# A fused cross-attention and routed feed-forward kernel: six small moves between the engines at once

## The reference, cut to what matters

```python
x = x + xattn(layernorm(x), ctx)        # x, ctx: (128 batches, 128 tokens, 256)
x = x + ffn(layernorm(x))
# xattn: 16 heads of 16; q = xn Wq + bq, k = ctx Wk + bk, v = ctx Wv + bv
#        softmax(q k^T / 4) v, then Wo, bo
# ffn:   logits = xn Wr + rb; e = argmax(logits) over 32 experts
#        y = relu(relu(xn W1[e] + b1[e]) W2[e] + b2[e]), hidden size 64
```

## Time and profile before

| | |
|---|---|
| three runs, median | 1183.46 us (1182.79 to 1188.08) |
| the profiled execution, its own time | 1188.65 us |
| its span, first to last instruction | 1186.8 us |
| mean granted TensorE clock | 0.975 of full speed |
| PE, DVE, POOL, ACT busy | 92%, 80%, 74%, 67% |
| block stage | up to about 957 us |
| page stage | about 964 us to the end |

### The profile page before, as it was taken

One profiled execution on the slowest core, in us unless ns is written; L12 is line 12 of the kernel. 1 busy time (PEld: TensorE's weight loads), 2 busy tenths in 40 slices (PEclk: granted clock), 3 DMA queues, 4 the chain that ended last, 5 costly groups with the idle time before them and its releaser, 6 DMA issues. The chain is left out here.

```text
span 1186.8 us, 38807 instructions
## 1 busy us (share of the span) xinstructions
PE 1090.2 (92%) x15164; PEld 817.5 (69%) x15164; DVE 946.0 (80%) x2360; ACT 799.1 (67%) x1860; POOL 875.5 (74%) x1709
## 2 busy tenths in 40 slices
PE   5999999999999999999999999999998539999992
PEld 4676777777777777777777777777776339888772
DVE  5688888888888888888888888888888538777672
ACT  4777777777777777777777777777775326566551
POOL 5467777777777777777777777777776547777776
PEclk9999999999999999999999999999999759999997
DMA  6516222522222222222222222222210146666650
GB/s 217 167 55 144 77 79 83 149 79 77 84 77 73 74 73 79 77 74 74 73 75 81 81 75 74 73 77 81 68 41 34 58 155 202 205 209 205 203 160 12
DMA packets 91282, 120.37 MB, mean 101 GB/s; under 512 B 14096, under 2 KB 74139, under 8 KB 90909
## 3 DMA queue, kind: packets, MB, share of 16 engines
q1 hardware_dynamic: 77278, 84.04, 25.7%
q0 software_dynamic: 13824, 33.85, 7.8%
HBM read 60.61 MB, written 59.31 MB: 101 GB/s over the span
## 5 line engine op out<-in xcount | busy, mean ns | idle before, releaser
L575 DVE TENSOR_REDUCE mx<-m 128x4 bf16<-128x512 f32 x512 | 323.7, 672 | 3.3 <-PE m L790 3.2
L462 ACT ACTIVATE arena<-sc 128x512 f32<-128x512 f32 x512 | 264.6, 603 | 47.1 <-PE sc L814 46.9
L424 POOL DMA_INDIRECT out<-arena x160 | 157.3, 983 | 61.2 <-issue 35.4
L396 POOL DMA_INDIRECT pages<-row,slot_i x128 | 129.7, 1014 | 57.1 <-issue 53.8
L805 PE MATMUL sc<-qk 32*128 32x256 f32 x2048 | 166.6, 396 | 0.7 <-DVE bo_s L680 0.5
L823 PE MATMUL pB<-arena 128*32 128x128 f32 x4096 | 158.6, 277 | 0.6 <-DVE row L584 0.6
L831 PE MATMUL pB<-wo_s,aT 128*128 128x288 f32 x512 | 149.5, 415 | 6.9 <-DVE aT L606 6.9
L823 PEld LDWEIGHTS pB<-arena 128*32 128x32 f32 x4096 | 99.1, 110 | 43.9 <-issue 42.4
L773 PE MATMUL pA<-cHi,wqkv 128*128 128x512 f32 x252 | 119.6, 476 | 9.5 <-DVE wqkv L648 9.5
L773 PE MATMUL pA<-xnT,wqkv 128*128 128x512 f32 x372 | 126.2, 447 | 0.0
L595 DVE STREAM_TRANSPOSE tr<-pB 128x512 f32<-128x512 f32 x128 | 91.5, 714 | 36.8 <-PE pB L823 35.1
(11 more groups left out here) (158 smaller groups left out, 2489.4 us busy)
## 6 DMA issues: line engine op xcount, KB each, us to landing
arena<-pages SPq DMA_DIRECT2D x160, 130.0 KB, 2.5
cT<-ctxT SPq DMA_DIRECT2D x64, 256.0 KB, 3.5
xs<-x_in SPq DMA_DIRECT2D x128, 128.0 KB, 2.2
pages<-empty SPq DMA_DIRECT2D x120, 130.0 KB
pages<-empty SPq DMA_DIRECT2D x1, 5200.0 KB, 19.9
out<-arena POOLq DMA_INDIRECT x160
w2s<-w SPq DMA_DIRECT2D x1, 2080.0 KB
qk<-w SPq DMA_DIRECT2D x1, 2064.0 KB, 8.5
```

Source lines behind the costliest of these rows:

```text
L396: pool.indirect_dma_start(pages, bass.IndirectOffsetOnAxis(slot_i[:, u:u + 1], 0), row[:, q % 4, u, 0:ROW], None, bounds_check=last_slot, ...
L424: pool.indirect_dma_start(out_rows, bass.IndirectOffsetOnAxis(pr[:, r, COL_TOKEN:COL_TOKEN + 1].bitcast(U32), 0), pr[:, r, X0:X0 + D], Non ...
L462: act.activation(pt[:, u % 2, g].rearrange("p i k -> p (i k)"), sc[g][:, :], ACT.Exp).then_inc(S["exp_out"], 1)
L575: ins = dve.tensor_reduce(mx[:, 32 * g:32 * g + 4], mb[i][:, :].rearrange("p (h k) -> p h k", h=4), AX.X, ALU.max)
```

## The change

1. **4+2 projection.** `project` takes a range of its six matmuls. In u=1 and u=2 four of them go ahead of `values` and two after `project_out`; in u=0 and u=3 it stays three and three.
2. **Another bank for the router.** The logits' transpose and the ranks, and what reads them, use sc[0] in place of sc[3]. `logits_transpose` waits for no exponential of its own any more (`values` ahead of it waits for the second), `ranks` for the first.
3. **The router's choice.** `best(s-1)` runs ahead of `residual` in u=1, no longer behind it. `stats1` takes batch 0 in u=0, 1 and 2 in u=1 and 3 in u=3, where it took 0, 1, and then 2 and 3 at the end of u=2.
4. **Inverse sums in PSUM.** `inv` is 16 columns of bank pB.
5. **Rounded context by ScalarE.** `context_hi` replaces GpSimd's cast: in u=0 behind `v_copy`, for block s+2. For block 0 it is ScalarE's first work, for block 1 it is in u=3 of s=-2.
6. **GpSimd's list.** `rstd1` goes to the head of a block, ahead of `scatter`. `slot_sum` writes integers itself (with max, as all but one of the slots' products are zero) into two buffers, so GpSimd's cast goes; `meta` is two instructions and no longer five.

```diff
+        inv = pB[:, 480:496]
...
-                pe.transpose(sc[3][:, 0:P], lgs[:, :], ident).then_inc(S["lgT_done"], 1)
+                pe.transpose(sc[0][:, 0:P], lgs[:, :], ident).then_inc(S["lgT_done"], 1)
...
             def split(q):
-                for c in range(2):
-                    pool.wait_ge(S[f"ld_c{c}"], q * 16 + 16)
-                if q >= 2:
-                    after(pool, "V_done", 4, q - 2, 3)
-                pool.tensor_copy(cHi[:, q % 2], cT[:, :, :]).then_inc(S["ctx_hi"], 1)
                 after(pool, "ctx_hi", 1, q, 0)
...
-                pool.tensor_scalar(expert[:, :], idx[:, :], -1.0, float(E), ALU.mult, ALU.add).then_inc(S["expert_out"], 1)
-                pool.tensor_copy(row[:, q % 4, :, COL_TOKEN].bitcast(I32), tok[:, :])
-                pool.tensor_copy(row[:, q % 4, :, COL_EXPERT].bitcast(I32), expert[:, :]).then_inc(S["meta_out"], 1)
-                pool.tensor_scalar(tok[:, :], tok[:, :], float(QB * P), None, ALU.add).then_inc(S["tok_out"], 1)
+                pool.tensor_scalar(row[:, q % 4, :, COL_TOKEN].bitcast(I32), cst[:, C_TOKEN:C_TOKEN + QB], float(q * QB * P), None, ALU.add)
+                pool.tensor_scalar(row[:, q % 4, :, COL_EXPERT].bitcast(I32), idx[:, :], -1.0, float(E), ALU.mult, ALU.add).then_inc(S["meta_out"], 1)
...
-                pool.tensor_copy(slot_i[:, :], slot[:, :]).then_inc(S["slot_int"], 1)
...
             for s in range(-1, NQ + 2):
+                if live(s + 2):
+                    rstd1(s + 2)
                 if live(s - 2):
-                    slots_as_integers(s - 2)
                     scatter(s - 2)
                 if live(s - 1):
                     rstd2(s - 1)
                     scale_logits(s - 1)
-                if live(s + 2):
-                    rstd1(s + 2)
...
+            def context_hi(q):
+                for c in range(2):
+                    act.wait_ge(S[f"ld_c{c}"], q * 16 + 16)
+                if q >= 2:
+                    after(act, "V_done", 4, q - 2, 3)
+                act.activation(cHi[:, q % 2], cT[:, :, :], ACT.Copy).then_inc(S["ctx_hi"], 1)
...
+                    if s == -2 and u == 3:
+                        context_hi(1)
+                    if u == 0 and s >= 0 and live(s + 2):
+                        context_hi(s + 2)
...
-                dve.tensor_reduce(slot[:, :], t1[:, :, :], AX.X, ALU.add).then_inc(S["slot_out"], 1)
+                dve.tensor_reduce(slot_i[:, q % 2, :], t1[:, :, :], AX.X, ALU.max).then_inc(S["slot_out"], 1)
...
-                    if u < 2 and live(s + 3):
-                        stats1(s + 3, (u,))
+                    if u != 2 and live(s + 3):
+                        stats1(s + 3, ((0,), (1, 2), (), (3,))[u])
...
+                    if u == 1 and live(s - 1):
+                        best(s - 1)
                     if live(q1):
                         residual(q1, u1)
-                    if u == 1 and live(s - 1):
-                        best(s - 1)
-                    if u == 2 and live(s + 3):
-                        stats1(s + 3, (2, 3))
...
-                        project(pq, n, (0, 1) if s < 0 else (0,))
+                        project(pq, n, 0, 6 if s < 0 else (3, 4, 4, 3)[u])
...
                     if u == 1 and s >= 0 and live(s + 1):
-                        after(pe, "exp_out", 16, s, 4 * u + 3)
                         logits_transpose(s + 1)
                     if u == 2 and live(s - 1):
                         if live(s):
-                            after(pe, "exp_out", 16, s, 4 * u + 3)
+                            after(pe, "exp_out", 16, s, 4 * u)
                         ranks(s - 1)
                     if live(q1):
                         project_out(q1, u1)
                     if live(pq) and s >= 0:
-                        project(pq, n, (1,))
+                        project(pq, n, (3, 4, 4, 3)[u], 6)
```

More of the change, by code:

```diff
@@ L120, in build @@
         t1 = sb("t1", [QB, E])
-        slot, slot_i = sb("slot", [QB]), sb("slot_i", [QB], U32)
-        tok, expert = sb("tok", [QB]), sb("expert", [QB])
+        slot_i = sb("slot_i", [2, QB], U32)
         empty = sb("empty", [ROW])
@@ L392, in scatter @@
                     pool.wait_ge(S[f"fill{q % 4}"], q // 4 * 64 + 64)
-                after(pool, "slot_int", 1, q, 0)
+                after(pool, "slot_out", 1, q, 0)
                 after(pool, "meta_out", 1, q, 0)
@@ L430, in _ @@
         def _(act):
+            def context_hi(q):
[4 more added lines that the diff above has]
+                act.activation(cHi[:, q % 2], cT[:, :, :], ACT.Copy).then_inc(S["ctx_hi"], 1)
+            context_hi(0)
             act.wait_ge(S["ld_wk"], 16)
@@ L628, in choose @@
                 if q >= 1:
-                    after(dve, "expert_out", 1, q - 1, 0)
+                    after(dve, "meta_out", 1, q - 1, 0)
                 own("idx_out", q + 1, dve.tensor_reduce(idx[:, :], eq[:, :, :], AX.X, ALU.max))
@@ L642, in slot_sum @@
                 if q >= 1:
-                    after(dve, "slot_int", 1, q - 1, 0)
-                dve.tensor_reduce(slot[:, :], t1[:, :, :], AX.X, ALU.add).then_inc(S["slot_out"], 1)
+                    after(dve, "scattered", 64, q - 1, 63)
+                dve.tensor_reduce(slot_i[:, q % 2, :], t1[:, :, :], AX.X, ALU.max).then_inc(S["slot_out"], 1)
             def low(w):
@@ L765, in transposes, with project @@
                 ins.then_inc(S["xnT_done"], 1)
-            def project(q, n, halves=(0, 1)):
+            def project(q, n, first, last):
                 c = n % 2
                 w = 1 if n < 2 else 0
[L770 to L775, removed]
+                for k in range(first, last):
+                    i, (a, b) = k // 3, HI_LO[k % 3]
+                    src = (cHi, cLo)[b][:, q % 2] if n < 2 else xnT[:, b]
+                    ins = pe.matmul(proj_bank(q, n)[:, :], wqkv[:, w, a, i, c * P:(c + 1) * P], src[:, i, :],
+                                    start=(k == 0), stop=(k == 5))
+                if last == 6:
                     ins.then_inc(S["proj_done"], 1)
@@ L846, in ranks @@
                 for v in range(QB - 1):
-                    pe.matmul(sc[3][:, (v + 1) * E:QB * E], ones_b[:, :], hot[:, v:v + 1].to_broadcast([P, QB - 1 - v, E]),
+                    pe.matmul(sc[0][:, (v + 1) * E:QB * E], ones_b[:, :], hot[:, v:v + 1].to_broadcast([P, QB - 1 - v, E]),
                               start=(v == 0), stop=False, skip_group_check=True)
-                pe.matmul(sc[3][:, 0:QB * E], tri_b[:, :], hot[:, :, :], start=False, stop=True, skip_group_check=True)
+                pe.matmul(sc[0][:, 0:QB * E], tri_b[:, :], hot[:, :, :], start=False, stop=True, skip_group_check=True)
                 for v in range(QB):
-                    ins = pe.matmul(sc[3][:, QB * E:(QB + 1) * E], ones_b[:, :], hot[:, v], start=False, stop=(v == QB - 1),
+                    ins = pe.matmul(sc[0][:, QB * E:(QB + 1) * E], ones_b[:, :], hot[:, v], start=False, stop=(v == QB - 1),
                                     skip_group_check=True)
@@ L891, in router_weights @@
                 after(pe, "lgs_out", 1, 0, 0)
+                pe.wait_ge(S["setup_copies"], 3)
                 logits_transpose(0)
@@ L972, in _ @@
                         if s == -1:
-                            pe.wait_ge(S["setup_copies"], 3)
+                            after(pe, "lg_out", 1, 0, 0)
                         after(pe, "xn_out", 2, s + 2, 0)
```

23 lines of the change are left out of this document (8 added, 15 removed).

## The result

The changed kernel takes 1147.89 us (median of 4 runs, 1147.08 to 1150.02), the kernel before 1185.77 (4 runs, 1182.79 to 1189.86): a ratio of 0.968, 95% interval 0.964 to 0.972. The forecast was 1145. The profiled execution took 1147.29 us where the sum gave 1150.5: 41.4 us gone where 38.2 were forecast. By the medians it is 37.9, as executions of the kernel before spread over 7 us and the profiled one was among the longer; what follows compares the two profiled executions.

The account below looks back on a forecast made before the run. TensorE, busy 92% of the span, sets the pace, so only its idle time can be won. Blocks 34.1 and statistics 5.8 us won, start +2.0, tail -0.3: 1183.46-38.2=1145.3; 8-in-10 range 1139 to 1163.

Parts of the forecast that it names:

- the sum: Whole kernel: block savings, statistics, start and tail added to -38.2 us, profiled execution from 1188.65 to 1150.5; chance 0.60.
- (a): `values` behind `project`, u=1 and u=2: TensorE idles for the second exponential, 0.22 us a step, 0.44 a block.
- (b): Fourth exponential holds up `logits_transpose` in u=1 (0.19 us) and `ranks` in u=2 (0.20): 0.39 a block.
- (c): `max_transpose` in u=2 waits for VectorE, 0.37 us too late; 0.27 a block counted as won.
- ScalarE's queue: `squares` and two query copies wait for `residual`, ahead of `mxT_copy`: 0.10 us a block taken off, bounds 0 and 0.32.
- (d): `max_transpose` in u=3 waits 0.37 us against 0.17, behind two statistics batches on VectorE: 0.20 a block.
- The start and the tail: Start 2.0 us later, once, behind ScalarE's conversion of block 1's context; tail 0.3 us shorter without GpSimd's cast.
- A: Rival: VectorE or ScalarE takes half of the gain; -23 us, 1160; chance 0.20.
- C: Rival: filled waits only move elsewhere, so the parts change nothing; 1175 to 1183 us; chance 0.07.
- D: Rival: late `z_out` delays `best` and `residual`, 1 us a block per us beyond 0.94; 1208 at 3 us; chance 0.05.

Follow-up runs that it names:

- the first experiment: Changed kernel with the projection back at three and three matmuls in all steps, against the changed kernel: 1157.74 us, block 27.35 us.

## Why the prediction was right, and where it wasn't

- **What bounds it, (a) and (b).** Right in place, and nearly in size: 0.43 and 0.33 by undoing, 0.44 and 0.39 forecast. The idle time of TensorE, and not the loader's longer wait, was the right measure; where the prediction took the loader's wait all the same, 0.20 for `ranks`, undoing shows 0.13. But the terms were taken as independent, and they aren't: alone in the kernel before the two parts win 0.26.
- **(c), the 0.37 us of `max_transpose` in u=2.** It was won in full: u=1 to 2 shrank by 0.80, and 0.22 + 0.19 + 0.37 is 0.78. The step's size was off by the 0.10 that I took off for ScalarE's queue; `mxT_copy` of u=2 follows its transposition by 0.29 as everywhere. But "`best` moves into the idling" is not what it hangs on: undone, it costs 0.09. The cast that stretched L617 (L622 of before) is gone as well, and either of the two nearly pays for (c): with the cast back and `best` ahead, u=1 to 2 takes 6.87 as in the changed kernel, and with the cast gone and `best` behind 6.98. Both undone together wasn't run, so how the 0.37 divides stays open.
- **L617 at 0.67, `best` at 0.97** (507.87 to 508.84). I took 0.8 between bounds 0.53 and 1.12. It ends 0.12 us after the end of the third subtraction of `split` (506.59 + 3 x 0.71 = 508.72, L617 at 508.84), as L622 ended 0.14 after the cast. In the experiment with `best` behind the residual it takes 0.29: it starts at 510.55, as GpSimd's last subtraction is about to end (507.86 + 2.80 = 510.66), so there is next to nothing to wait for. The Trainium skill, "SBUF — State Buffer", section "SBUF: two separate sides", has a lock for this: a VectorE instruction with two SBUF inputs and a GpSimd instruction that reads SBUF exclude each other for the whole instruction. The traces here agree, and the multiplication with one input in PSUM, at 420 to 423 ns in all 128 cases, escapes it.
- **(d), the statistics.** Forecast 0.20, measured 0.39 by undoing, though u=2 to 3 shrank by just the 0.62 forecast. The 0.20 was what the wait showed behind (a) and (b); remove those, and the same lateness costs 0.4.
- **The step that failed: GpSimd's list.** The prediction says of the factors at a block's head: "Not on the path in a block". Undoing it costs 0.54 us a block. That `norm1` would no longer wait for its factors it did say, but gave that no price, as in the trace of before the wait was hidden. The sum came out right all the same, as it was built from TensorE's idle times, all of which closed; but it ascribed them to four parts. Undone one at a time, the seven parts cost 0.43 + 0.33 + 0.09 + 0.39 + 0.10 + 0.14 + 0.54 = 2.02 us, more than the 1.45 won. They aren't additive: a wait that one part removes is in part hidden behind those that the others remove.
- **The inverse in PSUM, and ScalarE.** Priced at 0 with a worry about PSUM's cost; undoing it costs 0.10. The conversion took 1.048 us (1.15 forecast), and the gap before `mxT_copy` in u=1 is still 0.48, not 0.18: the conversion went into the gap ahead of `squares`, and the rest was absorbed because successive instructions overlap by some 0.1 (501.63 + 1.05 ends after 502.60).
- **The start and the tail.** +1.7 for +2.0, and -0.3 for -0.3. That the conversion causes the +1.7 is not shown: kernels with this same start have their first `max_transpose` anywhere from 34.5 to 38.1.
- **How much of the agreement is luck.** The blocks won 45.0 us where 39.9 were forecast; the odd step, which the sum left out, took 2.5 of that back. Forecast and measurement are nearer each other than their parts.
- **The rivals.** A didn't come: `max_transpose` waits 0.17 in every step, and `subtract_max` no longer than before. C fell by the first experiment as a statement on the changed kernel; its mechanism is what the two TensorE parts meet when they are alone. D's mechanism was seen in the last but one block and in the delayed `z_out`, and I priced each us beyond the spare time at 1 us: it was 1.55 for 1.84 in the one case and 0.48 for 0.93 in the other.
- **Missed altogether:** the 2.5 us of the odd step, which the trace of before had too, at 7.77 us. As it lasts from 7.9 to 12.8 us in kernels that don't touch it, the 2.5 can't be put down to the change.

## What to carry to other kernels

When one engine sets the pace, add up its idle times for the whole, but don't divide them among the edits from the trace of before: a wait shows only what is left behind the waits ahead of it, and here a part worth next to nothing alone was worth 15 us beside the others. Undo the parts one at a time in the finished kernel, and try them alone in the old one; the two answers differ, and the difference shows what hides what. Before moving a VectorE instruction with two SBUF inputs, lay GpSimd's instructions beside it; a small input in PSUM takes it out of that. A large background transfer is worth splitting up: here it gave some 4 us.

## What the runs showed of the hardware

**One transfer of 2 MB stops TensorE later.** In the changed kernel, TensorE's matmuls around 113 us:

```profile
111.53 0.40 PE L766 MATMUL pA<-cHi,wqkv 128*128 128x512 f32 x1
113.68 0.63 PE L757 MATMUL sc<-cst,xn 128*128 128x128 f32 x4 [1.75 <-ACT arena L453]
...
115.27 2.12 PE L824 MATMUL pB<-wo_s,aT 128*128 128x288 f32 x4
```

The exponentials named as the releaser had ended at 112.90, 0.78 us before. After the stop of 1.75 us the granted clock, 1.00 (the 2.4 GHz level) in the window ahead, has a mean of 0.83 over the step, so a part of it ran at the 1.2 GHz level, and four matmuls of `project_out` take 2.12 us in place of 1.14: both parts make up the 3.6 us over the usual 6.68. The same step is the odd one in all twelve traces with the single transfer. In four of them, the kernel before's included, the clock stays at 1.00 and it takes 7.8 to 8.5 us; in the other eight its mean is 0.73 to 0.84 and it takes 10.3 to 12.8. So of the 2.5 us between the two kernels 1.6 are the clock's (PE busy 8.50 us in place of 6.91) and the rest the longer stop. SP's own issues are slow in that stretch:

```profile
95.69 0.66 SPq L232 DMA_DIRECT2D w2s<-empty  x1
101.33 0.33 SPq L188 DMA_DIRECT2D xs<-x_in  x1
101.70 2.64 SPq L228 DMA_DIRECT2D pages<-empty  x1
108.14 0.33 SPq L188 DMA_DIRECT2D xs<-x_in  x1
108.51 2.47 SPq L228 DMA_DIRECT2D pages<-empty  x1
```

L228 usually takes 0.43. The step is gone in both kernels with the transfer split, and in the changed kernel TensorE goes on at 113.68, 0.6 us after the transfer has landed (95.69 + 17.4). That the large transfer causes it is shown; by what path it reaches TensorE (its instructions, which come by DMA too, or another late transfer) is only a guess.

**PSUM as a source is no slower here.** The multiplication of 256 elements takes 0.420 us with an input in PSUM and at least 0.424 with both in SBUF. The 62 cycles more that the errata section of "VectorE: DVE Perf Modes" in the Trainium skill gives PSUM sources don't show in this instruction.
